# Rotating halves first in the prologue, the first head's high parts handed over alone, and the small weights split in the first group

## The reference

```python
x = x + attn(layernorm(x))       # 16 heads of 64; the first 32 of q and k are rotated
x = x + ffn(layernorm(x))        # low rank: gelu((x @ U1) @ V1 + b1) @ U2 @ V2 + b2

# attn
q = h @ Wq; k, v = split(h @ Wkv)
q, k = rope(q), rope(k)          # y1 = x1*cos - x2*sin, y2 = x2*cos + x1*sin on 32 of 64
out = softmax(q @ k.T * 64 ** -0.5) @ v
return out @ Wout + bout
```

## Time and profile before

| | |
|---|---|
| median of 3 runs | 1410.24 us (1410.2 to 1410.78) |
| the profiled execution | 1414.48 us, of which its span 1412.4 us |
| TensorE busy | 1371.1 us, 97% of the span |
| DVE busy | 1167.9 us, 83% |
| POOL busy | 986.8 us, 70% |
| ScalarE busy | 785.5 us, 56% |
| granted TensorE clock, mean | 0.99 of full speed |

### The profile page before, as it was taken

One profiled execution on the slowest core, in us unless ns is written; L12 is line 12 of the kernel. 1 busy time (PEld: TensorE's weight loads), 2 busy tenths in 40 slices (PEclk: granted clock), 3 DMA queues, 4 the chain that ended last, 5 costly groups with the idle time before them and its releaser, 6 DMA issues.

```text
span 1412.4 us, 25020 instructions
## 1 busy us (share of the span) xinstructions
PE 1371.1 (97%) x7377; PEld 505.5 (36%) x7377; DVE 1167.9 (83%) x1308; ACT 785.5 (56%) x1506; POOL 986.8 (70%) x503
## 2 busy tenths in 40 slices
PE   3899999999999999999999999999999999999998
PEld 1233342333334233333433333343333334333344
DVE  7888888788887888888788887878889787898855
ACT  3365655556555555555555555555555555555666
POOL 4697878658585866858577685857768586787571
PEclk8899999999999999999999999999999999999999
DMA  6222031312203131220313222031222203122001
GB/s 200 54 46 60 17 83 39 75 32 60 60 15 82 38 70 35 60 60 15 82 38 66 39 60 60 15 82 38 62 43 57 63 15 82 39 46 60 16 16 61
DMA packets 72270, 75.63 MB, mean 54 GB/s; under 512 B 36036, under 2 KB 37576, under 8 KB 72104
## 3 DMA queue, kind: packets, MB, share of 16 engines
q1 hardware_dynamic: 71080, 70.89, 23.0%
q10 hardware_dynamic: 1152, 4.26, 0.8%
HBM read 22.04 MB, written 2.35 MB: 17 GB/s over the span
## 4 chain that ended last, share of the span: by engine, by line
PE 53%; issue 21%; POOL 15%; DVE 6%; ACT 2%; DMA 1%; POOLq 0%; SPq 0%; ACTq 0%; DVEq 0%
PE O L417 18%; PE S L405 10%; PE S L406 9%; POOL SA L707 6%; PE M L428 5%; POOL T L677 4%; PE TILE L359 3%; PE TILE L331 3%; POOL YR L680 2%; POOL STAGE L694 2%; DVE MX L628 2%; ACT PF L542 2%; PE TILE L347 1%; PE TILE L337 1%; DVE SUM L635 1%
## 5 line engine op out<-in xcount | busy, mean ns | idle before, releaser
L707 POOL TENSOR_TENSOR SA<-PF 128x1024 f32<-128x1024 f32 x255 | 655.9, 2579 | 353.3 <-DVE SUM L635 294.7
L542 ACT ACTIVATE PF<-S 128x512 f32<-128x512 f32 x1024 | 556.1, 597 | 443.3 <-PE S L406 441.7
L628 DVE TENSOR_REDUCE MX<-M 128x1 f32<-128x1024 f32 x510 | 599.8, 1217 | 157.2 <-PE M L428 156.0
L417 PE MATMUL O<-PF,V 128*64 128x512 f32 x2048 | 496.1, 605 | 0.0
L405 PE MATMUL S<-QK 128*128 128x512 f16 x1024 | 393.3, 384 | 3.6 <-ACT PF L542 3.6
L406 PE MATMUL S<-QK 128*128 128x512 f16 x1024 | 389.4, 380 | 0.0
L638 DVE TENSOR_TENSOR SUM<-SUM,SA 128x1024 f32<-128x1024 f32 x127 | 225.2, 1773 | 3.1 <-POOL SA L707 2.0
L417 PEld LDWEIGHTS O<-PF,V 128*64 128x64 f32 x2048 | 124.0, 136 | 247.0 <-issue 173.7
L405 PEld LDWEIGHTS S<-QK 128*128 128x128 f16 x1024 | 99.3, 97 | 254.1 <-issue 106.7
L428 PE MATMUL M<-QK 64*128 64x512 f16 x1020 | 161.6, 393 | 10.4 <-DVE MX L628 9.8
L406 PEld LDWEIGHTS S<-QK 128*128 128x128 f16 x1024 | 100.7, 98 | 48.2 <-issue 1.1
(11 more groups left out here) (130 smaller groups left out, 744.2 us busy)
## 6 DMA issues: line engine op xcount, KB each, us to landing
QK<-STAGE SPq DMA_DIRECT2D x128, 256.0 KB, 3.9
QK<-STAGE SPq DMA_DIRECT2D x128, 128.0 KB, 3.1
RB<-den SPq DMA_DIRECT2D x124, 128.0 KB, 3.0
QK<-MN SPq DMA_DIRECT2D x128, 1.0 KB, 2.0
out<-X SPq DMA_DIRECT2D x8, 256.0 KB, 2.0
RT<-DS SPq DMA_DIRECT2D x124, 2.0 KB, 1.7
X<-in_L_attn_queries ACTq DMA_DIRECT2D x3, 512.0 KB, 12.3
WRAW<-in_L_attn_Wkv ACTq DMA_DIRECT2D x2, 512.0 KB, 8.9
```

The source lines that it names most:

```text
L417: mm = e.matmul(O[DH * z:DH * z + DH, :], V[:, h, kt * DH:(kt + 1) * DH], PF[:, t % SLOTS, z * HALF:(z + 1) * HALF], start=(kt == 0), stop ...
L542: e.activation(PF[:, t % SLOTS, z * HALF:(z + 1) * HALF], S[:, z * HALF:(z + 1) * HALF], ACT.Exp, scale=EXP_SCALE).then_inc(exped, 1)
L628: e.tensor_reduce(MX[:, place % 2, q:q + 1], bank, AX, ALU.max).then_inc(max_read, 1)
L707: e.tensor_tensor(SA[:, (t // 2) % 2, :], PF[:, t % SLOTS, :], PF[:, t % SLOTS + 1, :], ALU.add).then_inc(two_summed, 1)
```

## The change

- The order of the projections: the four rotating tiles of q and k, then the four passing ones, then v. The ring of banks has eight places, with the four halves of M at its end.
- POOL does its three sums of rotated tiles first and then subtracts for all four; DVE does the fourth sum, not its subtraction. ScalarE's high copies of the rotating tiles stand behind the tiles 3, 4, 6 and 7.
- SP first hands over the high parts of the first head alone, in four DMAs on a new semaphore, handed_high, as soon as all high parts of a half are made; then that head's low parts, in four DMAs on handed[0]; then the other heads as before. TensorE's first unit waits for handed_high and for the passing low parts (whose banks in M the units overwrite); its loop begins with a wait for handed[0].
- DVE's ten maxima come right behind the low part of WV. The statistics of the second batch come behind the maxima.
- The small weights are split by DVE at step 23 of the first group.

```diff
--- before.py
+++ after.py
@@ -39,8 +39,7 @@
 PRE_CHUNKS = KT // CHUNK
 
 QK_TILES = [(w, c, t) for w in "qk" for c in range(2) for t in ("rot", "pass")]
-PROJ = [("q", 0, "rot"), ("q", 0, "pass"), ("q", 1, "rot"), ("q", 1, "pass"), ("k", 0, "rot"), ("k", 0, "pass"),
-        ("k", 1, "pass"), ("k", 1, "rot"), ("v", 0, 0), ("v", 0, 1)]
+PROJ = [(w, c, t) for t in ("rot", "pass") for w in "qk" for c in range(2)] + [("v", 0, c) for c in range(2)]
 QK_AT = (0, 2, 4, 7, 8, 10, 12, 14)
 V_AT = {16: (1, 0), 17: (1, 1), 24: (0, 0), 26: (0, 1)}
 DEN_AT = {6: 1, 20: 0}
@@ -195,7 +194,7 @@
         T = pb("TILE", [P, 512], F32)
         HB = [M[:, side, z * 512:(z + 1) * 512] for side in range(2) for z in range(2)]
         SH = [S[:, 0:512], S[:, 512:1024]]
-        PB = [T[:, :], S[:, 512:1024], O[:, :], S[:, 0:512]]
+        PB = [T[:, :], S[:, 512:1024], O[:, :], S[:, 0:512], HB[2], HB[3], HB[0], HB[1]]
         EARLY_T = [[PF[:, 2 + n, k * 512:(k + 1) * 512] for k in range(2)] for n in range(4)]
         EARLY_Y = [PF[:, 6 + n // 2, n % 2 * 512:(n % 2 + 1) * 512] for n in range(4)]
 
@@ -211,7 +210,7 @@
         rot_read, rot_parts, rot_sum, rot_hi, rot_lo = (sem(f"rot_{n}") for n in ("read", "parts", "sum", "hi", "lo"))
         pass_hi, pass_lo, v_made = sem("pass_hi"), sem("pass_lo"), sem("v_made")
         added = sem("added")
-        handed = [sem(f"handed{h}") for h in range(GH)]
+        handed, handed_high = [sem(f"handed{h}") for h in range(GH)], sem("handed_high")
         unit_made, max_read, max_found, max_row = (sem(n) for n in ("unit_made", "max_read", "max_found", "max_row"))
         scored, exped, pv_done, o_copied = sem("scored"), sem("exped"), sem("pv_done"), sem("o_copied")
         two_summed, summed = sem("two_summed"), sem("summed")
@@ -657,6 +656,8 @@
                     dve_max(e, it.step(v), it.i * GH + v // KT, (v // KT) % GH, v % KT, M[:, v % 2, :])
             dve_tiles(e, it, t)
             dve_ln(e, it, t)
+            if it.first and t == 23:
+                split_ff_weights(e)
             if t in INVERT_AT and not (it.first and INVERT_AT[t]):
                 dve_invert(e, it.pair(INVERT_AT[t]))
             if it.last and h == GH - 1 and kt in END_SUM_AT:
@@ -817,11 +818,19 @@
             sp.dma_start(WO[:, :, :], wout_d.rearrange("(c p) n -> p c n", p=P)).then_inc(wo_in, 16)
 
             sp.wait_ge(set_up, 3)
-            for h in range(GH):
-                sp.wait_ge(pass_lo, 4)
-                hand_over(sp, h, 1)
-                sp.wait_ge(rot_lo, 4)
-                hand_over(sp, h, 0)
+            for t in (1, 0):
+                sp.wait_ge((rot_hi, pass_hi)[t], 4)
+                sp.dma_start(QK[32 * t:32 * t + 32, 0, 0:3:2, :], STAGE[0:32, 1:3, t, :]).then_inc(handed_high, 16)
+                sp.dma_start(QK[DH + 32 * t:DH + 32 * t + 32, 0, 1:3, :],
+                             STAGE[0:32, 1:3, t, :]).then_inc(handed_high, 16)
+            for t in (1, 0):
+                sp.wait_ge((rot_lo, pass_lo)[t], 4)
+                for side in (0, 3):
+                    sp.dma_start(QK[DH + 32 * t:DH + 32 * t + 32, 0, side, :],
+                                 STAGE[0:32, side, t, :]).then_inc(handed[0], 16)
+            for h in range(1, GH):
+                for t in range(2):
+                    hand_over(sp, h, t)
             max_over(sp, 0, 0)
             loop(sp, sp_iteration)
             for c in range(FC):
@@ -848,6 +857,7 @@
             for nth in range(3):
                 pool.wait_ge(rot_parts, nth + 1)
                 pool.tensor_tensor(EARLY_Y[nth], EARLY_T[nth][0], EARLY_T[nth][1], ALU.add).then_inc(rot_sum, 1)
+            for nth in range(4):
                 early_low(pool, nth)
             ln_rstd(pool, 1)
 
@@ -908,11 +918,8 @@
             w_part(2)
             for n, args in enumerate(PROJ):
                 act_tile(act, "proj", args, n + 1, 0, PB[n % len(PB)])
-                if args in (("q", 0, "pass"), ("q", 1, "pass")):
-                    early_high(args[1])
-                elif args == ("k", 1, "pass"):
-                    early_high(2)
-                    early_high(3)
+                if n in (3, 4, 6, 7):
+                    early_high((3, 4, 6, 7).index(n))
             act.wait_ge(b1_turned, 1)
             act.activation(B1[:, :], M[:, 0, 0:FF // P], ACT.Copy).then_inc(b1_copied, 1)
 
@@ -979,8 +986,11 @@
             pe.wait_ge(b1_copied, 1)
             pe.wait_ge(set_up, 4)
             for u in range(LEAD):
-                if u % KT == 0:
-                    pe.wait_ge(handed[u // KT], HAND)
+                if u == 0:
+                    pe.wait_ge(pass_lo, 4)
+                    pe.wait_ge(handed_high, HAND)
+                elif u == KT:
+                    pe.wait_ge(handed[1], HAND)
                 wait(pe, max_read, u - 2 if u < KT else u - 1)
                 pe_unit(pe, u, u // KT, u % KT, first_bank(u))
 
@@ -990,6 +1000,7 @@
                         e.wait_ge(wo_in, 16)
                     pe_step(e, it, t)
 
+            pe.wait_ge(handed[0], HAND)
             loop(pe, body)
             def up(c):
 
@@ -1151,15 +1162,13 @@
                     dve.wait_ge(rot_parts, 4)
                     dve.wait_ge(rot_sum, 3)
                     dve.tensor_tensor(EARLY_Y[3], EARLY_T[3][0], EARLY_T[3][1], ALU.add).then_inc(rot_sum, 1)
-                    early_low(dve, 3)
-                    dve.wait_ge(w_hi, 5)
-                    dve.scalar_tensor_tensor(WV[:, 1, :], WRAW[:, 2, :], WSCALE, WV[:, 0, :], ALU.mult,
-                                             ALU.subtract).then_inc(w_lo, 1)
-            split_ff_weights(dve)
+            dve.wait_ge(w_hi, 5)
+            dve.scalar_tensor_tensor(WV[:, 1, :], WRAW[:, 2, :], WSCALE, WV[:, 0, :], ALU.mult,
+                                     ALU.subtract).then_inc(w_lo, 1)
+            for u in range(LEAD):
+                dve_max(dve, u, u // KT, u // KT, u % KT, first_bank(u))
             ln_stats(dve, 1)
             ln_aggr(dve, 1)
-            for u in range(LEAD):
-                dve_max(dve, u, u // KT, u // KT, u % KT, first_bank(u))
 
             def body(e, it):
                 for t in range(STEPS):
```

## The result

The changed kernel takes 1415.73 us (median of 9 runs, 1412.51 to 1418.86) against 1410.78 (median of 9, 1410.2 to 1415.74) for the kernel before on the same chip: a ratio of 1.0031, 95% interval 1.0020 to 1.0042. It is slower, by 2.8 to 5.9 us. The forecast was 1413.4 in a range of 1409.0 to 1416.0, with a chance of 0.52 for slower.

What follows compares the result with a forecast made beforehand. The prediction took TensorE, with 53% of the chain and hand-offs through other engines, to pace the kernel. 1.4 for late statistics plus 1.8, the mean of 1.9 (split) and 1.7 (clock), gave +3.2: 1410.24 to 1413.4, range 1409.0 to 1416.0.

Steps and rivals of the forecast that it cites:

- The start: Prologue: the first maximum at 33.6 against 35.07, with WV's low part held 0.9 us; units start 1.5 us earlier.
- The hand-over of high parts: Prologue DMAs: the last issued at about 26.5, landing near 30, before the unit's 33.0, so costing nothing.
- The statistics behind the units: POOL reaches the loop at 56.0; step 4's exponential is 1.7 late, TensorE's next score +1.4 us (bounds +0.5, +2.3).
- The split at step 23: First group: the multiplication by RB stands behind POOL's sum of pairs, delaying step 28's units by +1.9 us (bounds 0, 1.9).
- the additions: The split's 1.9 us and the clock's 1.7 us, each about an even chance; one taken as likeliest, at their mean, 1.8.
- the first rival: Whole kernel: both extra losses come, 1.4 + 1.9 + 1.7 = +5.0, 1415.2 us; chance 0.20.
- the first addition: Step 25: the split's 1.9 us, hanging on 0.4 us between RB's landing and the end of DVE's sum.
- The clock: After TensorE's 2.8 us stand at step 4 the granted clock may fall to 0.50, costing 0 to 1.7 us.
- the last rival: Prologue: units start at 35.07 as before, +2.9 at step 4, additions up to +6, 1413 to 1416.5; chance 0.08.
- The earlier start: Rival: the prologue's gain comes through whole, -1.5 to -2.4 us, 1408.8 to 1407.8; chance 0.12.
- its condition: For the prologue's gain to come through, POOL would have to be in the loop by 55.5.
- No earlier start: Rival: DVE's holds or a late hand-over leave the units at 35.07; 1413 to 1416.5; chance 0.08.

Runs made afterwards that it cites:

- stats_first: Changed kernel with the second batch's statistics back ahead of DVE's ten maxima, the split staying at step 23: 1412.6 us, ratio 1.0006 to the kernel before.
- before_stats_late: Kernel before with only the second batch's statistics moved behind the ten maxima: 1414.7 us, ratio 1.0023.
- before_split23: Kernel before with only the small weights' split moved to step 23 of the first group: 1412.32 us, ratio 1.0013.
- after_filled: Changed kernel with ten more matmuls on TensorE in its stand at step 4 of the first group: 1416.54 us, ratio 1.0030 to the kernel before.
- split_pro: Changed kernel with the small weights' split back in the prologue ahead of the maxima, the statistics staying behind them: 1413.57 us, ratio 1.0014 to the kernel before.
- reorder_only: Changed kernel with statistics and split both ahead of the maxima again, the new projection order kept: 1409.27 us, ratio 0.9979 to the kernel before.
- split_behind: As reorder_only, but with the small weights' split behind the ten maxima and ahead of the loop: 1409.97 us, ratio 0.9987 to the kernel before.
- split_pro_filled: split_pro with ten more matmuls on TensorE in its stand at step 4: 1415.63 us, ratio 1.0023 to the kernel before.
- a3_again: Changed kernel, unchanged, profiled a fourth time: one execution of 1419.36 us.
- stats_split21: stats_first with the small weights' split at step 21 of the first group for step 23: 1415.72 us, ratio 1.0030 to the kernel before.

## Why the prediction was right in its mechanism, and what it mis-sized

- **The start.** The first maximum came at 33.30 (predicted 33.6), WV's low part was held 0.8 us (0.9), the fourth sum took 1.52. The values' projection began at 29.17 against 30.88. Counted from the first rotating tile the start gained 1.5 to 1.7, for the 1.5 of the forecast. The hand-over of high parts stayed hidden: the last was issued at 26.07, and the units began at 32.65 without a wait for it. What the first profile shows beyond that at step 1 (-2.48) is mainly the clock's earlier rise.
- **The statistics behind the units.** Root 47.22 (47.5), first rotation 55.70 with no idle time before it (56.0), exponential of step 4 at 58.87 (59.3), so 1.29 late for the 1.7, TensorE's stand 3.08 (2.8), and TensorE's next score 1.04 late for the +1.4; from step 8 to step 24 it is 1.11 to 1.13. stats_first takes the loss away and before_stats_late makes it without the rest of the change: shown.
- **The split at step 23.** +1.70 for the +1.9. Its long multiplication came in all seven profiles with the split at step 23 (the changed kernel's four, stats_first, before_split23, after_filled), and in none of the six that have it ahead of the loop (that of before among them). In these seven the multiplication waited between 0.41 and 0.67 us for RB, so RB did land behind the end of DVE's sum, as predicted. But when DVE's sum ended, POOL's sum had also been standing for 1.1 us, and the row at 197.68 shows such an operation go first with RB there. So it isn't shown that the loss hung on RB's landing.
- **The choice between the additions was the step that failed.** Each was called an even chance and one of the two taken, +1.8 together. The split's loss came in 7 of 7, and the clock's fall in 3 of 4. The terms as they stand, 1.4 + 1.9 + 1.7 = 5.0, were the first rival's, with 1415.2 and a chance of 0.20; four profiles give 4.5 on the mean, and the timing gives 4.4. The error was to hang the first addition on a margin of 0.4 us and to take it as one that goes either way: it came out at 0.41 to 0.67, on the same side each time. The prediction had the other condition in its own rows, POOL's sum coming at 112.8 in the middle of DVE's sum from 112.29 to 113.9. The measured median lies 0.3 us below the upper end of the range, so the range held narrowly.
- **The clock.** The prediction let the clock fall because this stand is longer than the one near 1280. It fell, but length doesn't decide it: of the six profiles with an unfilled stand at step 4 it fell behind 2.21 (before_stats_late), 2.28, 2.44 and 3.01 us, and not behind the two longest, 3.07 (split_pro) and 3.08.
- **Its sums.** The sum of the rotation ends at 58.6 by the prediction's own terms, not at 58.65, and the last rival with both additions comes to 2.9 + 1.9 + 1.7 = 6.5, so 1416.7, not +6 and 1416.5. Nothing hangs on either.
- **The rivals.** The earlier start came through whole only where the statistics stayed ahead of the maxima and the split ahead of the loop (reorder_only, split_behind); POOL was then in the loop by 55.5, as its condition said. No earlier start: refuted by all four profiles.

The four repeats put a size on what the earlier trace rows showed once. The multiplication by RB comes about twice a group; where it misses its place before POOL's sum, what stands behind it is late. In the profile of before it does so near 1277, with the clock's fall behind it, and at 281 (DVE's timeline):

```profile
281.23 2.55 DVE L650 TENSOR_TENSOR OS<-OS,RB 128x1024 f32<-128x1024 f32 x1 [0.97 <-DMA RB<-den]
```

In the changed kernel the multiplication that answers to the second took 1.23. These two misses are why the profiled execution of before is the longer one: from +2.83 at step 30 to +1.64 at group 14 it loses 1.2 against the changed kernel's, and from there to the end (spans of 1412.4 and 1410.3, so -2.1) another 3.7. The miss near 1280 came in 10 of the 14 profiles, and not in the first of the changed kernel, reorder_only, before_split23 and before_stats_late: there the multiplication waited 0.37 to 0.84 us for RB, in the ten 0.95 to 1.82. In five of the ten the clock fell behind it (before, split_pro, split_behind, split_pro_filled, a3_again). From the start of the 15th group to that of the 16th these five lose 3.8 to 3.9 us against the changed kernel's first profile, and the five with the miss alone 2.2. So this place, behind the last column of the table, moves single executions by 2.2 or 3.9 us, with the change and without it; that it makes the spread of the other executions too was not tested by itself.

## What to carry to other kernels

A piece moved off one engine's path should be priced by the queue of the engine that reads its result: the statistics cost DVE nothing behind the maxima, but POOL runs in order, and its first rotation of the loop stood behind the work that waits for them. Before a piece is moved into the loop, look for idle time of the same engine where it already stands: DVE waited 4.23 us for the units in the changed kernel, and both pieces fit in there: with them back, step 30 came 2.7 us earlier than before (1.5 of it the change's) instead of 2.8 to 6.0 later. And where two additions hang on margins, order the events that meet (which starts first, which is delayed along with it) before calling a margin a coin's throw. When single executions are compared, count from a row ahead of the change: 0.5 us of a gain can stand there before the change has done anything.

## What the runs showed of the hardware that was not expected

- A stand of TensorE of 2.3 to 3.1 us let the granted clock fall from 1.00 to 0.50 in 3 of 4 executions of the same program, and not in the one with the longest stand (3.08 us; the others 2.28, 2.44 and 3.01). Two other kernels with the stand: a fall behind 2.21 us (before_stats_late), none behind 3.07 (split_pro). The same stand filled with ten matmuls let it fall in none of two, which is too few to tell from that.
- An operation of POOL that already stands beside a DVE operation goes ahead of DVE's next one, though that one is ready: the multiplication at 197.68 of the kernel before took 2.28 us for 1.21, and 2.28 to 2.29 in all 14 profiles.
- Short operations of DVE can be held for many times their own length. In stats_split21 three subtractions of 128x32 took 3.51 us, against 0.40 in the changed kernel. Two operations of POOL, of 2.62 and 1.33 us, which read two tensors each, lie on the same stretch (98.85 to 102.8), and the first and the third subtraction end 0.05 us behind one of them each, so all but some 0.4 us of the 3.51 was standing. The three operations ahead of them, with one tensor read, took 1.68 instead of 0.34. The Trainium skill (SBUF — State Buffer, "Who interferes with whom") says that a VectorE instruction with two SBUF inputs and a GpSimd instruction that reads SBUF lock each other out; the trace agrees for the subtractions, and shows that a row of short ones can pay it more than once.
